# Late projections, one memset fewer, and regrouped matrix products in a two-layer decoder kernel

## The reference

```
L0: mamba both ways | cross attention, 16 heads of 64 | 8 routed experts + a shared one
L1: causal attention, 16 heads, rank 32               | retention, 16 heads of 16 | experts by hash
```

```
cross:     scores = (x Wq)(ctx Wk)^T / 8, masked; attn = softmax(scores); out = attn (ctx Wv)
causal:    scores = (q Wq_lsr)(k Wk_lsr)^T / sqrt(32), lower triangle; y = softmax(scores) v
retention: sim = q k^T * gamma^(n-s) for n >= s; ret = sim v
```

## Time and profile before

| | |
|---|---|
| runs | 2788.98, 2792.68, 2798.53 us; median 2792.68 |
| profiled execution | 2785.95 us, its span 2784.2 us |
| PE busy | 2491.5 us (89%) |
| PEld busy | 1496.9 us (54%) |
| DVE busy | 1757.6 us (63%) |
| ACT busy | 1358.5 us (49%) |
| POOL busy | 1150.4 us (41%) |
| DMA | 227.22 MB, mean 82 GB/s |

### The profile page before, as it was taken

How to read it: one execution, slowest core, us unless ns; L and a number is a source line. 1 busy time by engine, 2 the same in 40 slices (tenths; PEclk the granted TensorE clock), 3 DMA queues, 4 the chain that set the end, 5 groups by cost and what they waited for, 6 DMA issues and landing times. The chain is left out here.

```text
span 2784.2 us, 47511 instructions
## 1 busy us (share of the span) xinstructions
PE 2491.5 (89%) x18594; PEld 1496.9 (54%) x18594; DVE 1757.6 (63%) x3457; ACT 1358.5 (49%) x2383; POOL 1150.4 (41%) x612
## 2 busy tenths in 40 slices
PE   5989989999997778999997799999889898788899
PEld 2334434344343334544444688999745455666557
DVE  2799899999999747787878531111336666465433
ACT  4566565665665246676666421111256666122231
POOL 2789889988889714333343201222210000200030
PEclk8999999999999988999999999999989999899999
DMA  5031130211303063444444325554220000200030
GB/s 218 1 129 57 65 137 2 121 73 64 122 21 146 10 175 71 82 100 82 85 78 115 105 100 180 180 188 169 78 66 1 1 1 1 92 9 1 1 108 31
DMA packets 126110, 227.22 MB, mean 82 GB/s; under 512 B 7904, under 2 KB 97504, under 8 KB 109760
## 3 DMA queue, kind: packets, MB, share of 16 engines
q1 hardware_dynamic: 122144, 213.95, 24.5%
q0 software_dynamic: 3744, 10.23, 1.0%
HBM read 201.74 MB, written 22.41 MB: 81 GB/s over the span
## 5 line engine op out<-in xcount | busy, mean ns | idle before, releaser
L208 POOL TENSOR_TENSOR m_h<-m_h,m_bc 128x1024 f32<-128x1024 f32 x256 | 612.4, 2413 | 79.0 <-DVE m_h L521 79.0
L521 DVE TENSOR_TENSOR_SCAN m_h<-m_da,m_h 128x1024 f32<-128x1024 f32 x256 | 578.8, 2278 | 42.6 <-ACT m_da L411 42.5
L281 PE MATMUL m_psy<-m_h,m_ident 128*128 128x512 f32 x1024 | 493.2, 614 | 23.6 <-POOL m_h L208 23.6
L411 ACT ACTIVATE m_da<-x_rows,m_a_neg 128x511 f32<-128x511 f32 x512 | 330.7, 680 | 153.9 <-DVE m_h L521 150.5
L937 POOL TENSOR_SCALAR c_pr<-c_pr,c_share 128x512 f32<-128x512 f32 x128 | 200.4, 1565 | 377.0 <-DVE c_share L1215 377.0
L281 PEld LDWEIGHTS m_psy<-m_h,m_ident 128*128 128x128 f32 x1024 | 196.4, 197 | 291.6 <-issue 235.0
L508 DVE TENSOR_TENSOR m_h<-m_dtx,m_bc 128x1024 f32<-128x1024 f32 x192 | 232.2, 1210 | 24.1 <-PE m_psy L281 17.7
L983 PE MATMUL c_psS<-c_kT,c_qT 64*128 64x512 f32 x512 | 152.1, 672 | 44.2 <-DVE c_low L1207 43.3
L227 PE MATMUL m_rot<-early_ctx,early_w 128*128 128x512 f32 x240 | 132.8, 682 | 62.4 <-ACT m_gz L387 44.1
L1098 ACT ACTIVATE c_pr<-c_pr,c_low 128x512 f32<-128x512 f32 x256 | 180.9, 707 | 2.9 <-DVE c_low L1207 2.7
L1104 ACT ACTIVATE c_pr<-c_pr,c_share 128x512 f32<-128x512 f32 x128 | 92.3, 721 | 159.9 <-DVE c_share L1215 159.4
(11 more groups left out here) (396 smaller groups left out, 4068.0 us busy)
## 6 DMA issues: line engine op xcount, KB each, us to landing
m_bc<-bc_dram SPq DMA_DIRECT2D x32, 2048.0 KB, 7.7
e_up<-in_up SPq DMA_DIRECT2D x39, 1024.0 KB
c_vr<-v_dram SPq DMA_DIRECT2D x128, 256.0 KB, 5.0
v_dram<-c_stage SPq DMA_DIRECT2D x32, 256.0 KB, 2.3
e_down<-in_down SPq DMA_DIRECT2D x8, 1024.0 KB
e_down<-y_dram SPq DMA_DIRECT2D x8, 512.0 KB, 8.1
h_w<-in_w SPq DMA_DIRECT2D x2, 2048.0 KB, 14.1
m_taps<-in_taps SPq DMA_DIRECT2D x1, 2560.0 KB, 11.9
```

The source lines that it names most:

```text
L208: pool.tensor_tensor(hq, hq, bc[:, 1, NP * s:NP * (s + 1), :], ALU.mult).then_inc(p_ready, 1)
L281: mm = pe.matmul(bank, ident[:], h[:, n % HB, e, :], start=False, stop=(s == NG - 1 and e == NP - 1))
L411: ins = act.activation(da[:, n % 2, e, at:at + L - 1], dt[:, u, j, at:at + L - 1], ACT.Exp, scale=a_neg[:, u, j, NP * s + e:NP * s + e + 1])
L521: dve.tensor_tensor_scan(flat, decay, flat, 0.0, ALU.mult, ALU.add).then_inc(scanned, 1)
```

## The change

1. Cross attention, first sequence: `FIRST` is cut from 24 projections to 12 (all v; k and q of head pairs 0 and 7), and `LATE` puts k and q of pairs 1 to 5 into iterations 0 to 9 and of pair 6 into 12 and 13, as an `extra` in `psX`, emptied by ACT. `scores` of a pair wait until its late q is kept. The load of the third sequence's context moves from before SP's loop to its iteration 13.
2. The memset in front of the second head goes, in cross and in causal attention.
3. Causal attention: `attend` for blocks 0 and 1 comes together in iteration 1 of a group, for 2 and 3 in iteration 3.
4. Retention: the three products with the state come first, then all sixteen small ones.

```
-        FIRST = [(what, m) for m in range(NM) for what in "kv"] + [("q", m) for m in range(NM)]
-        NKV = 2 * NM
+        FIRST = [("k", 0)] + [("v", m) for m in range(4)] + [("k", 7)] + [("v", m) for m in range(4, NM)] + [("q", 0), ("q", 7)]
+        NKV = NM + 2
+        LATE = {2 * m - 2 + s: (what, m) for m in range(1, 6) for s, what in enumerate("kq")}
+        LATE.update({12: ("k", 6), 13: ("q", 6)})
...
                     if b == 2:
-                        sp.wait_ge(first_full, NKV)
+                        sp.wait_ge(x_full, numbers[12] + 1)
...
-                load_ctx(2)
                 for n in range(TOTAL):
...
+                    if n == 13:
+                        load_ctx(2)
...
+                    elif b == 0 and u in LATE:
+                        mm = project(psX[:], 0, *LATE[u])
...
+                        elif u % LT == 0 and u // LT < 7:
+                            pe.wait_ge(x_free, numbers[2 * (u // LT) - 1 if u // LT < 6 else 13] + 1)
...
+                    dve.memset(spare[:, 13 * (n % 2):13 * (n % 2) + 1], 0.0)
                     for i in range(2):
-                        dve.memset(spare[:, i + 13 * (n % 2):i + 13 * (n % 2) + 1], 0.0)
...
                         if o < LT:
-                            attend(q, o)
+                            if o % 2 == 1:
+                                attend(q, o - 1)
+                                attend(q, o)
...
+                    dve.memset(spare[:, 2 * (n % 2):2 * (n % 2) + 1], 0.0)
                     for i in range(2):
                         at = 2 * (n % 2) + i
-                        dve.memset(spare[:, at:at + 1], 0.0)
...
+                    for c in range(1, LT):
+                        pe.matmul(psO[:, c * P:(c + 1) * P], state[:, c - 1, m, :], padT[:, 1, m, c * P:(c + 1) * P],
+                                  start=(c == 1), stop=False, skip_group_check=True)
                     for c in range(LT):
-                        if c >= 1:
-                            pe.matmul(psO[:, c * P:(c + 1) * P], state[:, c - 1, m, :], padT[:, 1, m, c * P:(c + 1) * P],
-                                      start=True, stop=False, skip_group_check=True)
                         for i in range(HM):
                             mm = pe.matmul(psO[PAD * i:PAD * (i + 1), c * P:(c + 1) * P], v[:, b % 2, c, HM * m + i, :],
-                                           sim[:, m % 2, i, c, :], start=(c == 0), stop=True, skip_group_check=True)
+                                           sim[:, m % 2, i, c, :], start=False, stop=True, skip_group_check=True)
```

More of the change, by code:

```diff
@@ L822, in cross_attention_stage @@
             if 1 <= b < NB and u in BEHIND:
+                numbers[n] = len(numbers)
+            elif b == 0 and u in LATE:
                 numbers[n] = len(numbers)
@@ L1126, in keep_extra @@
                         return
-                    use = BEHIND[u] if b >= 1 and u in BEHIND else AHEAD[u]
-                    to = b if b >= 1 and u in BEHIND else b + 1
+                    own = BEHIND if b >= 1 else LATE
+                    use, to = (own[u], b) if u in own else (AHEAD[u], b + 1)
                     act.wait_ge(x_full, numbers[n] + 1)
```

## The result

The changed kernel took 2758.62 us (median of 4 runs, 2755.16 to 2762.79) against 2791.19 us for the kernel before beside it; the ratio is 0.988, 95% interval 0.9858 to 0.9902. So the change is faster, by 0.9 to 1.2%. Between the medians timed beside each other the gain is 32.6 us in the first timing and 24.3 in the second: the side is right, the gain is larger than forecast, and the first median lies at the lower edge of the range. The profiled execution took 2759.56 us (span 2757.8), 26.4 less than the profiled execution before.

What follows compares the result with a forecast made beforehand. The prediction took PE as the bound, except the first cross loop, where PE idles waiting on DVE. Terms -3.3 - 1 - 3 - 13 = -20.3 us took 2785.95 to 2765.7, plus 6.7 gave 2772; range 2758 to 2785.

Steps and rivals of the forecast that it cites:

- What bounds the kernel: Cross attention's start, causal attention and retention: PE sets the pace; first cross loop: 20 us idle PE between DVE waits.
- Part 1: Late projections in cross attention: loop starts 11 us earlier and gives back 7.7; net -3.3 us, between -15 and +12.
- (a): First cross loop: `scores(4)` wait for the second late projection, kept behind both exponentials of unit 3; 2.4 us.
- (b): First cross loop, iterations 3 to 9: projections wait for `psX` and hold up the next scores; together 2.6 us.
- (c): First cross loop, iterations 12 and 13: PE needs 7.97 us against DVE's 5.28; costs 2.7 us.
- Part 2: Cross and causal attention: removed memsets hide behind the reduce; 1 us gained in all, between 0 and 4.
- Part 3: Causal values in pairs: 4.5 us gained with projections between, 1.6 lost without; net -3 us, between -7 and +2.
- Part 4: Retention, states first: an `attend` takes 1.85 us instead of 2.66, 16 times; 13 us gained, between 7 and 15.
- the conversion: Whole kernel: 6.7 us, the shown median's excess over the profiled execution, added to 2765.7 to give 2772.
- fuller front: Rival, cross attention: front gives back all 21 us, 7 lost in the loop; -14 us, time 2761; chance 0.14.
- Small groups: Rival, retention: small-product groups keep their 0.35 us each; gain 5 to 7 us, time 2779; chance 0.13.
- serialise the loop: Rival, first cross loop: late projections cost 3.9 us each, 47 us for twelve; time 2812; chance 0.05.

Runs made afterwards that it cites:

- the experiment with the stores: Changed kernel with all eight stores of v issued ahead of the first reloads on SP's queue: 2752.07 us, ratio 0.9852.
- The experiment with two memsets: Kernel before with a second one-column memset ahead of each reduce in cross and causal attention: 2795.48 us, ratio 1.0022.
- memsets alone: Kernel before with only the second head's memset removed in cross and causal attention: 2789.6 us, ratio 0.9999.
- the experiment with three changes of shape: Changed kernel with retention's small products of block 0 first, then three state products, then the other small ones: 2765.28 us, ratio 0.9893.
- the second trace of the kernel before: Kernel before, unedited, run again as a kernel of its own: 2790.09 us, ratio 1.0004.
- the second timing: Changed kernel, unedited, timed again beside the kernel before on one chip with other kernels: 2763.78 us, ratio 0.9906.
- the product of the parts: Kernel before with each of the change's four parts by itself, in four separate runs; their ratios multiplied give 0.9913.

## Where the prediction held, and the step that failed

**What bounds the kernel** held: the parts that moved the time are the three that changed PE's work or its waits, and the one that took work off DVE did not.

**Part 1** has the right waits in the right places. The front gave 11.1 us where 11 was forecast: q starts 3.4 us sooner in the stretch (forecast 3.0), six q fewer give their 10.5, and 2.6 us are lost to the clock (forecast 2.5; the experiment with the stores gives them back). The loop gave back 7.5 (forecast 7.7), though by its steps differently: by the first reduces of unit 4, 12 and 16, (a) took 2.9 us for 2.4, (b) 1.4 for 2.6, (c) 4.2 for 2.7, and 1.1 us came back between (b) and (c). That the loop's sum came out within 0.2 us is luck: three terms were off by up to 1.5 us, and one was not there. For (a) the reason was half right: behind the exponentials stands the scaling of unit 2, which waits for DVE.

**Part 2** is right: 0.62 us with and without the memset, and nothing in the total. The experiment with two memsets adds that it is the place that counts, behind a reduce or in front of one.

**Part 3** has the right mechanism for both kinds of group, and nearly the size: -0.69 us where -0.56 was forecast, +0.15 where +0.2 was, with two of the groups with projections at no gain. By the groups at full clock this makes some 3.5 us. The causal part differs by 7.3 us between the first two traces, and the remainder goes by the clock: five other traces with the old order of products put that part at 366.4 (memsets alone), 367.4, 369.6, 372.1 and 374.7 us, and the eight with pairs lie between 361.4 and 366.6.

**Part 4 is the step that failed, by its size**: "a gain of 0.81, 16 times: 13 us". The attend gained 0.83, as said, but retention gained 16.6 to 17.2 us against the first trace in every trace with the edit (264.5 to 265.1 us in seven traces, against 281.7 to 282.1 in five of the six of the old order). The sum counted the changes of shape within an attend and left out the one at its entry: in three of four head pairs it follows a pick, and pick to state has one shape. That is 0.09 x 12 = 1.1 us; the experiment with three changes of shape brings it back. With it 16 x 0.83 + 1.1 = 14.4.

Another 1.7 us lie behind the last attend of the stage, in instructions that the change does not touch. These are that end in the kernel before, in the changed kernel, and in the one with three changes of shape; the columns are those of the windows above.

```profile
2654.84:2674.11 19.27, 14.47 (x48) 0.91 0.00 0
```

```profile
2630.15:2647.72 17.57, 12.77 (x48) 1.00 0.00 0
```

```profile
2637.25:2656.52 19.27, 14.46 (x49) 0.91 0.00 0
```

It is 19.24 to 19.27 us at a clock of 0.91 in all six traces of the old order and in the one with three changes of shape, and 17.57 to 17.59 at 1.00 in all seven with the states in front. So this fall of the clock is not chance: it comes and goes with the order of the products in the attends. It also closes the account of the experiment with three changes of shape: 4.1 + 1.7 = 5.8 of the 6.0 us. By what way the order reaches the clock there stays open. Of the 16.6 to 17.2 us this leaves 0.5 to 1.1 that I can't assign; the sum had no term for the entry and none for the clock.

**The sum against the median.** By stretches the four parts gave about -3.6, 0, -3.5 and -17, together -24, where -20.3 was forecast: part 4 gave 4 us more than its term and part 2 one less. The other 9 to 10 of the 13.4 us (2772 to 2758.6) come of the conversion and the scatter, which is argued from the numbers that follow and can't be split further. The forecast added the 6.7 us by which the shown median stood above the profiled execution. That was a draw of that one execution: the profiled one was 3 us above the median in the second trace of the kernel before, and 1 us above it in both of the changed kernel's timings. And the second timing puts the changed kernel itself 5 us higher than the first. The forecast of -20.3 as a ratio, 0.9927, lies just outside the second interval (0.9887 to 0.9925) and near the product of the parts, 0.991.

**The rivals.** The fuller front did not happen in the change (the wait of ACT grew to 8.92 us); it happened when the stores were put first, by the way the rival named. Small groups did not keep their 0.35 us: 32 of them take 1.02. Late projections did not serialise the loop: twelve cost 7.5 us, 0.6 each, far from the 3.0 at which the sign turns.

## What to carry to other kernels

Count the changes of array shape along PE's whole order of work, the entry and the exit of a reordered group too, and price them all alike: the same price held for six removed and for two put back. Then compare the code behind the reordered part as well: here it was 1.7 us shorter without being touched. When work is taken out in front of a wait, look for what the wait itself hangs on; here a store behind five loads in a queue held 7 us, and the idle time it made took another 2.6 through the clock. Don't carry the offset between one profiled execution and a median over to a forecast, and take a small part from its own rows, since a total with the clock's scatter can't tell 3 us in 2790.

## What the runs showed of the hardware that I had not expected

- Many stretches of lower clock come in other places in each execution of the same code: groups of 15.2 to 15.4 us take 16.1 to 16.3 at a granted clock of 0.89 or 0.90, and the same stretch of cross attention took 489.23 us at 0.99 and 495.19 at 0.97. At 0.97 it also took 489.8 to 492.0 in other runs, so the mean clock does not account for all of it.
- One such stretch does not wander: the end of retention is at 0.91 in the seven traces with seven or three changes of shape in an attend and at 1.00 in the seven with one, 1.7 us apart.
- A change of shape costs 0.14 to 0.15 us on PE, for six taken out as for two put back.
- Two memsets between two reduces cost 0.01 us; the same one in front of a reduce that DVE had waited for costs 0.03.
- A PE idle for 7.94 us did the next two projections in 6.29 us; idle for 1.00 us it did them in 3.70.
